# A convolution group by group beside the deformable gathers of the next image

## The chip, the cores and the metric

One core of one Trainium2 chip runs the whole program. The metric is the device time of one execution in microseconds (us); the median of several executions is compared.

## The reference

Four residual layers run over x of shape (4, 64, 128, 128): each adds to x a function of its group norm (32 groups of 2 channels, statistics over one image).

```python
x = x + L0(gn(x), ...)      # attention along columns
x = x + L1(gn(x), ...)      # deformable 3x3 convolution
x = x + L2(gn(x), ...)      # 3x3 convolution whose weights are drawn: w = loc + L eps
x = x + L3(gn(x), ...)      # five steps with position-dependent 3x3 filters
```

The change concerns L1 and L2. L1 computes, by a 3x3 convolution, 27 numbers for each pixel: an offset (dy, dx) and a mask for each of nine taps. Each tap is sampled at its displaced position by bilinear interpolation of four neighbours, and the 9 x 64 samples are contracted with the weight to 64 channels. L2 is an ordinary 3x3 convolution with zero padding, of 64 to 64 channels, plus a bias:

```python
w = weight_loc + einsum('oiab,oib->oia', L, eps_w).reshape(O, I, K, K)
out = conv(x, w, padding='SAME') + b[None, :, None, None]
```

## The kernel before

Everything is float32 here. The program is a sequence of blocks; in each block every engine has its own instruction stream, ordered by semaphores, and between blocks all engines meet at a barrier. `deformable` (L1) and `convolution` (L2) stand one behind the other: `deformable` writes x2 to DRAM, `group_norm(env, 2)` makes scale and shift of each image from the moments, `convolution` reads x2 and writes x3. Each works through the images b = 0 to 3, and each image in G = 32 groups of four image rows (512 pixels).

**The deformable stage.** For each image a table in DRAM holds, for every pixel of the padded image, the channels of two rows and of two columns, so that one gather of 1 KB brings the four neighbours. For each group:

- `params(g)`: TensorE convolves the normalised padded image `dc_xp` with the offset weights (`convolve`, L1292: six matmuls, which the trace lists as twelve passes, since a float32 matmul goes in two) into `dc_pc`; ScalarE copies it out with the bias (L1469); TensorE turns it so that pixels are on partitions (L1516); VectorE makes table indices and weights in 15 small steps (L1588 to L1609), ScalarE the mask (L1472).
- `consume(g)`: GpSimd issues, for each of the four image rows r, nine indirect DMAs (L1447), one per tap, into the row's own buffer `gt[:, r]`. Ahead of rows 0 and 2 stands a one-element addition (`dc_gate`, L1445), behind waits for VectorE's products of the two rows of the group before, whose buffers are filled anew. VectorE multiplies the gathered values with the weights (L1621, one instruction per row, `sampled[r]`). TensorE turns the products back with matmuls against the identity, which also sum the four neighbours (L1529: 20 matmuls a row, 40 in the trace). ScalarE copies the five banks out (L1483), and TensorE contracts them with the filter (L1541, five matmuls, ten in the trace) into `dc_po`. VectorE adds the raw rows of x1 (L1628), takes statistics (L1631, L1633), and SP stores the result to x2 (L1417).

The order is written out by hand in `pairs`: each engine runs `params(g + 1)` ahead of `consume(g)`. For images 1 to 3 the table is made in pieces beside the gathers of the image before: in every second group SP loads raw rows (`dc_nx`, L1380), ScalarE normalises them (L1478), TensorE turns them (L1539), and SP stores the piece (L1398). At a change of image SP loads the next image into `dc_xp` (`load_image`, L1375 and L1376), VectorE normalises it (L1574), and the last group's `consume` follows.

SP's queue in a group holds, in this order: the raw rows of the next group, the wait for the group's output, its store, and in even groups the table's stores and the load of the next piece.

**The convolution.** `bayes_weights` computes the drawn weights in a block of its own. Then whole images are loaded into two padded buffers `cv_xp`, in which partitions 64 to 127 hold the image shifted by one row; ScalarE normalises an image in place (L1782); TensorE convolves group by group into two banks of `cv_po` (L1292); VectorE adds bias and raw rows (L1808) and takes statistics (L1812, L1814); SP loads the raw rows (L1765) and stores x3 (L1769).

## Time and profile before

| | |
|---|---|
| median of 3 runs | 17333.0 us (17320.24 to 17361.81) |
| the profiled execution | 17346.83 us, span 17345.0 us |
| busy in the span | TensorE 73%, weight loads 41%, VectorE 55%, ScalarE 32%, GpSimd 50% |
| mean granted TensorE clock | 0.837 |
| attention and what is ahead of it | up to 6058 us |
| deformable stage | 6061 to 12082 us |
| group norm 2, drawn weights | 12083 to 12123 us |
| convolution | 12124 to 13048 us |
| filters (L3) | 13048 us to the end |

Times are those of one profiled execution, from the start of its span. PE is TensorE, DVE VectorE, ACT ScalarE, POOL GpSimd, SP the engine that only issues DMAs; PEld is the loading of matmul weights. A value in brackets at the end of a row of the timeline is the time that the engine stood idle ahead of it, and what ended that.

### The profile page before, as it was taken

How to read it: one execution, taken by the hardware profiler on the slowest of the kernel's cores; microseconds unless marked ns; L12 is line 12 of the kernel's file. 1: busy time of each engine (PE TensorE's matmuls, PEld its weight loads, DVE VectorE, ACT ScalarE, POOL GpSimd, SP SyncE). 2: the span in 40 equal slices, each digit the busy share in tenths (PEclk: the TensorE clock that was granted, in tenths of full speed). 3: DMA queues.
4: the chain of work that ended last, by engine and by line, in shares of the span. 5: the costliest groups of instructions: out<-in, count | busy, mean ns of one | idle time of the engine just before them, and what ended most of it. 6: DMA issues, size and time to landing. Idle time of an engine off the chain costs nothing. (4 is left out here: it accounts for less than half of the span.)

```text
span 17345.0 us, 233377 instructions
## 1 busy us (share of the span) xinstructions
PE 12681.1 (73%) x80914; PEld 7160.2 (41%) x80914; DVE 9531.3 (55%) x14944; ACT 5526.5 (32%) x7813; POOL 8648.0 (50%) x8027
## 2 busy tenths in 40 slices
PE   5554378888880057767767776776688999999998
PEld 2553145555550045555555555554223333333333
DVE  4556878888883423333333333333126777777777
ACT  1112444444440000000000000000106777777776
POOL 0112411111111057777777777776006777777777
PEclk9999976666665578888888888887899999999999
DMA  4113333333325954454454444333422021110201
GB/s 98 36 28 67 86 60 53 56 54 53 56 50 161 203 149 126 125 135 126 125 139 121 125 125 128 111 110 103 85 60 39 20 49 22 32 37 20 49 21 31
DMA packets 1324675, 1419.97 MB, mean 82 GB/s; under 512 B 514353, under 2 KB 1065537, under 8 KB 1308545
## 3 DMA queue, kind: packets, MB, share of 16 engines
q1 hardware_dynamic: 1031872, 755.61, 21.0%
q0 software_dynamic: 221184, 604.27, 12.1%
q10 hardware_dynamic: 70976, 50.83, 0.9%
q8 instruction: 488, 8.00, 0.2%
q14 instruction: 155, 1.26, 0.0%
HBM read 1049.46 MB, written 276.84 MB: 76 GB/s over the span
## 5 line engine op out<-in xcount | busy, mean ns | idle before, releaser
L1447 POOL DMA_INDIRECT dc_g<-corners,dc_idx x4608 | 4387.1, 952 | 1366.7 <-issue 1326.4
L1529 PE MATMUL dc_ps<-ident,dc_s 128*128 128x128 f32 x20480 | 2861.0, 311 | 1373.2 <-DVE dc_s L1621 1373.2
L2074 POOL TENSOR_TENSOR df_sq<-df_sq 128x512 f32<-128x512 f32 x1920 | 2519.2, 1324 | 1945.3 <-ACT df_sq L2022 1900.1
L1529 PEld LDWEIGHTS dc_ps<-ident,dc_s 128*128 128x128 f32 x20480 | 2813.9, 226 | 1410.8 <-issue 758.9
L2169 DVE SCALAR_TENSOR_TENSOR df_pr<-df_pk,vecs,df_h 128x512 f32<-128x512 f32 x2880 | 2092.8, 742 | 613.1 <-PE df_pk L1963 343.7
L2022 ACT ACTIVATE df_sq<-df_pk,vecs 128x512 f32<-128x512 f32 x2880 | 1936.0, 685 | 979.2 <-DVE df_pr L2169 956.3
L1621 DVE TENSOR_TENSOR dc_s<-dc_g,dc_pt 128x2304 f32<-128x2304 f32 x512 | 1296.5, 2552 | 1652.7 <-DMA dc_g<-corners,dc_idx 1158.6
L756 POOL TENSOR_TENSOR at_md<-at_mt,at_own 64x512 bf16<-64x512 f32 x256 | 327.5, 1279 | 2663.0 <-DVE at_mt L975 2663.0
L1483 ACT ACTIVATE dc_st<-dc_ps 128x512 f32<-128x512 f32 x640 | 327.0, 607 | 4146.6 <-PE dc_ps L1529 4146.6
L1960 PE MATMUL df_pk<-df_t,df_wp 64*128 64x512 f32 x3840 | 1351.0, 641 | 213.9 <-ACT df_sq L2022 156.7
L949 DVE SCALAR_TENSOR_TENSOR at_x<-at_pq,hconst,at_x 128x256 f32<-128x256 f32 x2048 | 1114.7, 617 | 371.9 <-PE at_pq L793 213.9
L1971 PE MATMUL df_py<-df_pr,df_pair 128*64 128x512 f32 x3840 | 1015.5, 669 | 1.7 <-DVE df_pr L2169 1.7
L1628 DVE TENSOR_TENSOR dc_xo<-dc_po,dc_raw 64x512 f32<-64x512 f32 x128 | 87.4, 683 | 1562.3 <-PE dc_po L1541 1562.3
L1960 PEld LDWEIGHTS df_pk<-df_t,df_wp 64*128 64x128 f32 x3840 | 491.0, 188 | 1011.4 <-ACT df_sq L2022 622.2
L1292 PE MATMUL cv_po<-cv_xp,cv_w 128*64 x1536 | 680.7, 600 | 277.1 <-DVE cv_xo L1808 169.0
L1963 PE MATMUL df_pk<-df_t,df_ws 128*128 128x512 f32 x1920 | 875.4, 592 | 0.0
L1004 ACT ACTIVATE at_x<-at_prr 128x512 f32<-128x512 f32 x1024 | 575.5, 597 | 520.3 <-PE at_prr L851 520.3
L982 DVE TENSOR_TENSOR at_x<-at_pt,at_x 128x512 f32<-128x512 f32 x1024 | 673.8, 678 | 108.4 <-PE at_pt L812 104.0
L1292 PE MATMUL dc_pc<-dc_xp,dc_wp 128*32 (+1 forms) x1536 | 692.4, 601 | 43.4 <-DVE dc_base L1576 42.7
L383 PE MATMUL as_py<-wqkv,as_w 64*128 64x128 f32 x2048 | 479.9, 426 | 310.1 <-DVE as_w L423 310.1
L967 DVE TRANSPOSE_TENSOR_REDUCE at_mx<-at_x 128x16 f32<-128x512 f32 x1024 | 687.4, 690 | 0.0
L851 PE MATMUL at_prr<-at_a,at_rel 96*128 96x128 bf16 x4096 | 564.7, 302 | 84.8 <-DMA at_a<-y 52.1
(273 smaller groups left out, 16781.8 us busy)
## 6 DMA issues: line engine op xcount, KB each, us to landing
df_h<-df_h SPq DMA_DIRECT2D x160, 512.0 KB, 7.1
dc_g<-corners,dc_idx POOLq DMA_INDIRECT x4608
corners<-dc_xt SPq DMA_DIRECT2D x90, 512.0 KB, 4.8
at_a<-y SPq DMA_DIRECT2D x192, 192.0 KB
dc_xp<-x SPq DMA_DIRECT2D x32, 1024.0 KB, 20.0
cv_xp<-x SPq DMA_DIRECT2D x8, 4096.0 KB, 49.8
y<-sp_p SPq DMA_DIRECT2D x128, 192.0 KB, 2.8
y<-sp_p SPq DMA_DIRECT2D x64, 384.0 KB, 4.3
```

Source lines behind the costliest of these rows:

```text
L949: last = nc.vector.scalar_tensor_tensor(out=x2, in0=pq[:, t % 2, 256 * i:256 * i + 256].rearrange("p (e b) -> p b e", e=2), scalar=env.hco ...
L967: nc.vector.tensor_reduce(mx[:, q % 2, 16 * t:16 * t + 16], x4.rearrange("p (a c) -> p a c", c=32), AX.X, ALU.max, apply_transpose=True).t ...
L1292: last = nc.tensor.matmul(out, weights[:, i, :], xp[:, bass.ds(row + ky, 4), kx:kx + W], start=(i == 0), stop=(i == 5))
L1447: nc.gpsimd.indirect_dma_start(gt[:, r, k, :, :].rearrange("p a c -> p (a c)"), None, image, bass.IndirectOffsetOnAxis(ap=idx[:, s, r, k:k ...
L1529: t = nc.tensor.matmul(ps[:, j, 128 * r:128 * r + 128], sm[:, r % 2, a, 2 * j:2 * j + 2, :].rearrange("p k c -> p (k c)"), env.ident[:, :] ...
L1621: nc.vector.tensor_tensor(sm[:, r % 2, :, 0:KK, :].rearrange("p a k c -> p k a c"), gt[:, r, :, :, :], w, ALU.mult).then_inc(sampled[r], 1)
L1960: nc.tensor.matmul(pk[:, j % BANKS, :], wp[p, k // 2, :], t[p, n % 2, :], start=True, stop=True, tile_position=(64 * (k % 2), 0)).then_inc ...
L1963: nc.tensor.matmul(pk[:, j % BANKS, :], ws[:, k - 6, :], t[:, n % 2, :], start=True, stop=True).then_inc(tapped, 1)
L1971: nc.tensor.matmul(py[64 * s:64 * s + 64, :], pair[:, :], pr[:, (KK * n + k) % RING, :], start=(k < 2), stop=False, tile_position=(0, 64 * s))
L2022: nc.scalar.activation(sq[:, j % RING, :], pk[:, j % BANKS, :], ACT.Square, bias=env.vecs[:, bias:bias + 1]).then_inc(squared, 1)
L2074: nc.gpsimd.tensor_tensor(a, a, sq[:, (KK * n + other) % RING, :], ALU.add).then_inc(nadded, 1)
L2169: nc.vector.scalar_tensor_tensor(out=rows(pr[:, j % RING, :]), in0=rows(pk[:, j % BANKS, :]), scalar=env.vecs[:, bias:bias + 1], in1=shift ...
```

## The change

- x2 gets 131 rows of DRAM per channel, H + 3: row 0 and the last two hold zeros, stored by twelve DMAs at the head of the deformable stage.
- `bayes_weights` runs ahead of the deformable stage.
- The deformable stage convolves image b - 1 beside the gathers of image b (b = 1 to 3), one group of four rows in each group, from row buffers `cvx` of two times six rows. The outputs use partitions 64 to 127 of `dc_po`, `dc_xo`, `dc_raw` and `dc_now`, of which only 0 to 63 were in use.
- At the end of each image its group norm 2 is computed: VectorE's moments, one matmul, a root on ScalarE, scale and shift on VectorE.
- `convolution` is left with image 3, which it loads and normalises in quarters.
- In `pairs` the first pair of groups of an image is written out ahead of the loop.

```diff
         def pairs(eng, b, params, consume, early=lambda b: None, late=lambda b: None):
             if b == 0:
                 params(0, 0, 0)
-            with eng.Fori(0, NP - 1) as i:
+            params(b, 1, 1)
+            consume(0, 0, 0)
+            params(b, 2, 0)
+            consume(1, 1, 0)
+            with eng.Fori(1, NP - 1) as i:
...
 SP
+            for b in range(B):
+                for y in (0, H + 1, H + 2):
+                    sp.dma_start(x2[b, :, y, :], zero[0:64, 0, :]).then_inc(z_stored, 16)
+                    n += 1
...
+                def load_conv(g, s):
+                    for half in range(2):
+                        sp.dma_start(cvx[64 * half:64 * half + 64, s, :, 1:W + 1],
+                                     x2[bass.ds(b - 1, 1), :, bass.ds(4 * g + half, 6), :].rearrange("o c h w -> (o c) h w")
+                                     ).then_inc(cv_in[s], 16)
+                    sp.dma_start(raw[64:128, s, :], x2[bass.ds(b - 1, 1), :, bass.ds(4 * g + 1, 4), :]
+                                 .rearrange("o c h w -> (o c) (h w)")).then_inc(craw_in[s], 16)
+
+                if b:
+                    for s in range(2):
+                        sp.wait_ge(out_st[s], 16 * b * G // 2)
+                    for s in range(2):
+                        load_conv(s, s)
...
                 def consume(g, s, i):
                     sp.wait_ge(o_out, b * G + g + 1)
...
+                    if b:
+                        sp.wait_ge(cv_out, (b - 1) * G + g + 1)
+                        sp.dma_start(x3[bass.ds(b - 1, 1), :, bass.ds(4 * g, 4), :].rearrange("o c h w -> (o c) (h w)"),
+                                     xo[64:128, s, :]).then_inc(cv_st[s], 16)
+                        if not isinstance(g, int) or g + 2 < G:
+                            load_conv(g + 2, s)
...
 ScalarE, consume
+                    if b:
+                        if isinstance(g, int) and g == 0:
+                            act.wait_ge(gn_ready, b)
+                        act.wait_ge(cv_in[s], 16 * (n - G - s) + 32)
+                        t = nc.scalar.activation(cvx[:, s, :, 1:W + 1], cvx[:, s, :, 1:W + 1], ACT.Identity, bias=gsh2[:, b - 1:b],
+                                                 scale=gsc2[:, b - 1:b])
...
+                        t.then_inc(cv_normed, 1)
...
 TensorE, consume, behind the turning of row r
                         t.then_inc(turned[r], 1)
+                        if r == 1 and b:
+                            pe.wait_ge(cv_normed, n - G + 1)
+                            pe.wait_ge(cv_out, n - G)
+                            convolve(nc, po[64:128, :], wst, cvx[:, s, :, :], 0).then_inc(cv_done, 1)
...
                 pairs(pe, b, params, consume)
+                pe.wait_ge(moments, b + 1)
+                nc.tensor.matmul(pt[:, 416:418], env.gavg[:, :], env.mv[:, b, :], start=True, stop=True).then_inc(summed, 1)
...
 VectorE, consume, behind the product of row 3
+                    if b:
+                        k = n - G
+                        dve.wait_ge(cv_done, k + 1)
+                        dve.wait_ge(craw_in[s], (k - s) * 8 + 16)
+                        dve.wait_ge(cv_st[s], (k - s) * 8)
+                        nc.vector.scalar_tensor_tensor(out=xo[64:128, s, :], in0=po[64:128, :], scalar=bias[64:128, 0:1],
+                                                       in1=raw[64:128, s, :], op0=ALU.add, op1=ALU.add).then_inc(cv_out, 1)
+                        dve.wait_ge(cv_out, k + 1)
+                        dve.wait_ge(cv_kept, k)
+                        nc.vector.bn_stats(now[64:128, s, :], xo[64:128, s, :]).then_inc(cv_stated, 1)
+                        dve.wait_ge(cv_stated, k + 1)
+                        nc.vector.tensor_scalar(st[64:128, b - 1, :][:, bass.ds(g * 6, 6)], now[64:128, s, :], 1.0, None, ALU.mult
+                                                ).then_inc(cv_kept, 1)
                     dve.wait_ge(o_done, n + 1)
...
                 pairs(dve, b, params, consume, late=normalise)
+                dve.wait_ge(kept, (b + 1) * G)
...
+                c.run(nc.vector.bn_aggr(env.mv[0:64, b, :], st[0:64, b, :]))
+                c.run(nc.vector.tensor_copy(env.mv[64:128, b, :], env.mv[0:64, b, :]))
+                c.run(nc.vector.tensor_tensor(gn[:, 0:1], mean, mean, ALU.mult))
+                nc.vector.tensor_tensor(var, var, gn[:, 0:1], ALU.add).then_inc(moments, 1)
+                dve.wait_ge(summed, b + 1)
...
 convolution, for image 3 alone
+            for q in range(4):
+                rows = x2[b, :, 32 * q + 1:32 * q + 33, :]
+                sp.dma_start(xp[0:64, 32 * q + 1:32 * q + 33, 1:W + 1], rows).then_inc(x_in[q], 16)
+                sp.dma_start(xp[64:128, 32 * q:32 * q + 32, 1:W + 1], rows).then_inc(x_in[q], 16)
...
+            for q in range(4):
+                pe.wait_ge(normed, min(3 * q + 6, 12))
+                for i in range(4 * q, 4 * q + 4):
                     for s in range(2):
-                        pe.wait_ge(o_out, b * G + 2 * i)
+                        pe.wait_ge(o_out, 2 * i)
...
 program
-        deformable(env, x1, ins["pgw"], ins["dcw"], table, x2)
-        env.layer_done()
-        group_norm(env, 2)
...
+            bayes_weights(env, ins, wst, bias[:, :])
+            deformable(env, x1, ins["pgw"], ins["dcw"], table, x2, wst, bias, st, gsc2, gsh2, x3)
+            env.layer_done()
+            convolution(env, x2, x3, wst, bias, st, gsc2, gsh2)
```

## Rows read from the trace of the kernel before

**Rows 1.** The page's costliest groups: count, busy us, mean ns, idle before

```profile
L1447 POOL DMA_INDIRECT dc_g<-corners,dc_idx x4608 | 4387.1, 952 | 1366.7 <-issue 1326.4
```

**Rows 2.** Busy us by stretch; last three: TensorE clock, DMA share, GB/s

```profile
6200.00:12060.00 5860.00, 4261.55 (x24418) 3268.27 (x24419) 1915.02 (x3073) 491.84 (x982) 4422.97 (x4852) 0.85 0.44 124
12127.00:12178.00 51.00, 0.00 (x0) 0.00 (x0) 0.06 (x1) 0.62 (x1) 0.00 (x0) 0.50 0.99 174
...
8346.00:8348.00 2.00, 2.00 (x12) 2.00 (x11) 0.00 (x0) 0.00 (x0) 1.70 (x2) 0.50 0.36 115
```

**Rows 3.** Timeline of GpSimd, gates in image 1: start, us, instruction

```profile
8316.77 0.18 POOL L1445 TENSOR_TENSOR dc_gate<-dc_gate 1x1 f32<-1x1 f32 x1
...
8339.35 0.18 POOL L1445 TENSOR_TENSOR dc_gate<-dc_gate 1x1 f32<-1x1 f32 x1
```

**Rows 4.** All gates: min/median/max ns, first and last start

```profile
L1445 POOL TENSOR_TENSOR dc_gate<-dc_gate x256: 182/183/236, 6185.5 to 12037.7; 1x1 f32<-1x1 f32 x128
```

**Rows 5.** Timeline of TensorE in ordinary groups of image 1

```profile
8355.91 5.34 PE L1292 MATMUL dc_pc<-dc_xp,dc_wp 128*32 x12
...
8389.02 6.36 PE L1529 MATMUL dc_ps<-ident,dc_s 128*128 128x128 f32 x40 [4.65 <-DVE dc_s L1621]
```

**Rows 6.** Timeline of TensorE behind the second and third change of image

```profile
9120.87 8.25 PE L1292 MATMUL dc_pc<-dc_xp,dc_wp 128*32 128x512 f32 x12 [14.09 <-DVE dc_base L1576]
...
9161.87 5.34 PE L1292 MATMUL dc_pc<-dc_xp,dc_wp 128*32 x12
...
9202.24 5.34 PE L1292 MATMUL dc_pc<-dc_xp,dc_wp 128*32 x12
...
10638.48 5.34 PE L1292 MATMUL dc_pc<-dc_xp,dc_wp 128*32 x12
...
10677.12 5.34 PE L1292 MATMUL dc_pc<-dc_xp,dc_wp 128*32 x12
```

**Rows 7.** Timeline of VectorE in image 1, the last during an image load

```profile
8311.23 0.68 DVE L1628 TENSOR_TENSOR dc_xo<-dc_po,dc_raw 64x512 f32<-64x512 f32 x1 [12.61 <-PE dc_po L1541]
...
8321.88 5.02 DVE L1621 TENSOR_TENSOR dc_s<-dc_g,dc_pt 128x2304 f32<-128x2304 f32 x2
...
9090.77 2.55 DVE L1621 TENSOR_TENSOR dc_s<-dc_g,dc_pt 128x2304 f32<-128x2304 f32 x1 [18.61 <-DMA dc_g<-corners,dc_idx]
```

**Rows 8.** Timeline of the weights' block and the convolution

```profile
12086.29 0.36 SPq L1669 DMA_DIRECT2D bw_L<-in_l_L  x1
...
12123.61 0.17 DVE L1271 MEMSET cv_xp<- 64x130 f32 x1 [0.92 <-PEq L1661]
...
12177.38 14.85 ACT L1782 ACTIVATE cv_xp<-cv_xp,gsh,gsc 128x16256 f32<-128x16256 f32 x3 [59.00 <-DMA cv_xp<-x]
...
12310.68 10.51 PE L1292 MATMUL cv_po<-cv_xp,cv_w 128*64 x24 [0.94 <-DVE cv_xo L1808]
...
12322.12 8.36 PE L1292 MATMUL cv_po<-cv_xp,cv_w 128*64 x19 [0.94 <-DVE cv_xo L1808]
```

**Rows 9.** All outputs of the convolution: ns, first and last start

```profile
L1808 DVE SCALAR_TENSOR_TENSOR cv_xo<-cv_po,cv_bias,cv_raw x128: 742/743/745, 12225.5 to 13042.2; 64x512 f32<-64x512 f32 x128
```

**Rows 10.** Timeline of the head of the deformable stage

```profile
6062.34 0.62 SPq L1375 DMA_DIRECT2D dc_xp<-x  x1
...
6101.23 15.50 SPq L1391 DMA_DIRECT2D corners<-dc_z  x24
...
6112.54 3.04 DVE L1574 TENSOR_SCALAR dc_xp<-dc_xp,gsc,gsh 128x3968 f32<-128x3968 f32 x3 [7.99 <-DMA dc_xp<-x]
```

**Rows 11.** Groups of instructions at the end of the stage

```profile
L1645 DVE BATCH_NORM_AGGREGATE mv<-dc_stat 64x2 f32<-64x192 f32 x4 | 3.7, 970 | 0.0
```

**Rows 12.** DMA issues, 8113 to 8203: count, KB, median us to landing

```profile
dc_nx<-x SPq DMA_DIRECT2D x2, 128.0 KB, 6.5
```

**Rows 13.** Timeline behind the first change of image, VectorE and GpSimd

```profile
7694.69 5.02 DVE L1621 TENSOR_TENSOR dc_s<-dc_g,dc_pt 128x2304 f32<-128x2304 f32 x2
...
7707.14 0.18 POOL L1445 TENSOR_TENSOR dc_gate<-dc_gate 1x1 f32<-1x1 f32 x1
```

More of the change, by code:

```diff
@@ L1291, in convolve, with deformable @@
         ky, kx = i // 3 * 2, i % 3
-        last = nc.tensor.matmul(out, weights[:, i, :], xp[:, bass.ds(row + ky, 4), kx:kx + W], start=(i == 0), stop=(i == 5))
+        last = nc.tensor.matmul(out, weights[:, i, :], xp[:, row + ky:row + ky + 4, kx:kx + W] if isinstance(row, int) else xp[:, bass.ds(row + ky, 4), kx:kx + W], start=(i == 0), stop=(i == 5))
     return last
-def deformable(env, x1, pgw, dcw, table, x2):
+def deformable(env, x1, pgw, dcw, table, x2, wst, bias, st, gsc2, gsh2, x3):
     nc = env.nc
@@ L1324, in deformable @@
         wp, wd = sb("dc_wp", [128, 6, 32]), sb("dc_wd", [128, 5, C])
-        zero = sb("dc_z", [65, 2, 128])
+        zero = sb("dc_z", [128, 2, 128])
+        cvx = sb("dc_cvx", [128, 2, 6, PW])
+        gn = sb("dc_gn", [128, 4])
         off = sb("dc_off", [128, 512])
@@ L1475, in consume @@
                     n = b * G + g
+                    if b:
[4 more added lines that the diff above has]
+                                                 scale=gsc2[:, b - 1:b])
+                        if isinstance(g, int) and g in (0, G - 1):
+                            t.then_inc(edge, 1)
+                            act.wait_ge(edge, 2 * b - 1 if g == 0 else 2 * b)
+                            y = 0 if g == 0 else 5
+                            t = nc.scalar.activation(cvx[0:64, s, y, 1:W + 1], zero[0:64, 0, :], ACT.Copy)
+                            if g:
+                                t = nc.scalar.activation(cvx[64:128, s, 4:6, 1:W + 1], zero[64:128, :, :], ACT.Copy)
+                        t.then_inc(cv_normed, 1)
                     if more and s == 0:
@@ L1540, in consume @@
                             t.then_inc(piece_turned, 1)
-                        t = nc.tensor.matmul(po[:, :], wd[:, j, :], stt[:, j, :], start=(j == 0), stop=(j == 4))
+                        t = nc.tensor.matmul(po[0:64, :], wd[:, j, :], stt[:, j, :], start=(j == 0), stop=(j == 4))
                     t.then_inc(o_done, 1)
@@ L1555, in _ @@
             c.add(nc.vector.memset(sm[:, :, :, KK, :], 0.0))
+            c.add(nc.vector.memset(cvx[:, :, :, 0:PW:PW - 1], 0.0))
             for r in range(4):
@@ L1627, in consume @@
                     dve.wait_ge(out_st[s], (n - s) * 8)
-                    nc.vector.tensor_tensor(xo[:, s, :], po[:, :], raw[:, s, :], ALU.add).then_inc(o_out, 1)
+                    nc.vector.tensor_tensor(xo[0:64, s, :], po[0:64, :], raw[0:64, s, :], ALU.add).then_inc(o_out, 1)
                     dve.wait_ge(o_out, n + 1)
                     dve.wait_ge(kept, n)
-                    nc.vector.bn_stats(now[:, s, :], xo[:, s, :]).then_inc(stated, 1)
+                    nc.vector.bn_stats(now[0:64, s, :], xo[0:64, s, :]).then_inc(stated, 1)
@@ L1632, in consume @@
                     dve.wait_ge(stated, n + 1)
-                    nc.vector.tensor_scalar(st[:, :, :].rearrange("p b f -> p (b f)")[:, bass.ds(n * 6, 6)], now[:, s, :], 1.0, None, ALU.mult).then_inc(kept, 1)
+                    nc.vector.tensor_scalar(st[0:64, b, :][:, bass.ds(g * 6, 6)], now[0:64, s, :], 1.0, None, ALU.mult).then_inc(kept, 1)
                 pairs(dve, b, params, consume, late=normalise)
-            dve.wait_ge(kept, B * G)
-            c = Steps(dve, link, start + B * G * (PARAM + CONSUME))
@@ L1641, in full_moments @@
+                assert c.n == 7
+                nc.vector.scalar_tensor_tensor(out=gsh2[:, b:b + 1], in0=gn[:, 1:2], scalar=-1.0, in1=gsc2[:, b:b + 1],
+                                               op0=ALU.mult, op1=ALU.mult).then_inc(gn_ready, 1)
+                dve.wait_ge(gn_ready, b + 1)
 def full_moments(env, c, st):
@@ L1644, in full_moments @@
     for b in range(B):
-        c.add(nc.vector.bn_aggr(env.mv[0:64, b, :], st[:, b, :]))
+        c.add(nc.vector.bn_aggr(env.mv[64:128, b, :], st[64:128, b, :]))
     c.wait()
-    c.run(nc.vector.tensor_copy(env.mv[64:128, :, :], env.mv[0:64, :, :]))
+    c.run(nc.vector.tensor_copy(env.mv[0:64, :, :], env.mv[64:128, :, :]))
 def bayes_weights(env, ins, wst, bias):
@@ L1711, in _, with convolution @@
             c.wait()
-def convolution(env, ins, x2, x3):
+def convolution(env, x2, x3, wst, bias, st, gsc2, gsh2):
     nc = env.nc
     G = H // 4
-    x_in = [env.sem("cv_x_loaded0"), env.sem("cv_x_loaded1")]
+    b = B - 1
+    x_in = [env.sem(f"cv_x_loaded{q}") for q in range(4)]
     normed, link, conv_done, o_out, stated, kept = (
@@ L1796, in _ @@
             c = Steps(dve, link)
[L1797 to L1798 removed]
+            clear_borders(nc, xp, c)
             nc.vector.memset(now[:, :, :], 0.0).then_inc(cleared, 1)
             dve.wait_ge(cleared, 1)
[L1801 to L1816 removed]
+            with dve.Fori(0, G // 2) as i:
+                for s in range(2):
+                    n = 2 * i + s
+                    dve.wait_ge(conv_done, n + 1)
+                    dve.wait_ge(raw_in[s], (n - s) * 8 + 16)
+                    dve.wait_ge(out_st[s], (n - s) * 8)
+                    nc.vector.scalar_tensor_tensor(out=xo[64:128, s, :], in0=po[64:128, s, :], scalar=bias[64:128, 0:1],
+                                                   in1=raw[64:128, s, :], op0=ALU.add, op1=ALU.add).then_inc(o_out, 1)
+                    dve.wait_ge(kept, n)
+                    dve.wait_ge(o_out, n + 1)
+                    nc.vector.bn_stats(now[64:128, s, :], xo[64:128, s, :]).then_inc(stated, 1)
+                    dve.wait_ge(stated, n + 1)
+                    nc.vector.tensor_scalar(st[64:128, b, :][:, bass.ds(n * 6, 6)], now[64:128, s, :],
+                                            1.0, None, ALU.mult).then_inc(kept, 1)
+            dve.wait_ge(kept, G)
             full_moments(env, c, st)
```

117 lines of the change are left out of this document (52 added, 65 removed).

## The prediction, made before the change was run

> **What bounds the kernel now.** I read the page first: the costliest group of all is GpSimd's gathers, 4608 of 0.95 us, with 1326 us in which the engine only issued, 0.29 us for each [rows 1]. They fill the deformable stage, 6.2 to 12.06 ms. Busy shares don't tell what sets its pace: TensorE is busy 4262 of 5860 us there, GpSimd 4423 [rows 2]. So next comes the timeline of GpSimd alone. Each half group (two of its four image rows) is opened by a small gate instruction (L1445) and holds 18 gathers; the gates stand 22.58 us apart [rows 3], 45.15 us a group, and 18 x (0.95 + 0.29) with the gate is just that: GpSimd does nothing else and waits for nobody. There are 256 gates from 6185.5 to 12037.7 [rows 4]. I went through all of them: every step has 22.6 us but those at the three changes of image. 255 x 22.58 = 5758 of 5852 us, so each change loses 31. GpSimd's issue is the bound.
>
> How far behind is TensorE? In an ordinary group it stops 4.65 us ahead of its last 40 turning matmuls, for VectorE's product of row 3, which waits for the gathered data [rows 5]. Just behind a change of image it runs without that stop, and its own period can be read: 10638.48 to 10677.12 is 38.6 us, and 9161.87 to 9202.24, a group that also turns a piece of the next table, 40.4 us [rows 6]. So TensorE's chain (offset convolution, ScalarE, turn, VectorE's 15 small steps, product of row 0, 160 turning matmuls, ScalarE's copies, ten matmuls of the filter) has 5 to 6.5 us to spare. VectorE is done with rows 0 and 1 at 8326.90 and GpSimd wants their buffers at 8339.35: 12 us of slack there [rows 3, 7].
>
> Behind the stage nothing overlaps. The weights begin at 12086.3, the convolution's block at 12123.6 [rows 8]; its first output is made at 12225.5, its last at 13042.2 [rows 9]. Two groups take 11.44 us (12310.68 to 12322.12), 5.72 each: twelve passes of TensorE and the handover with VectorE [rows 8].
>
> **The change, part by part.**
>
> *The tail.* Three of four images leave this block; the fourth is loaded in quarters. Such quarters of a padded image are loaded at the head of the deformable stage: issued from 6062.34, VectorE starts on the fourth at 6112.54, 50.2 us later [rows 10]. ScalarE takes 14.85 us for a whole image in three instructions [rows 8], so some 4 for a quarter, and TensorE can start on the first quarters well ahead of that. The raw rows for the addition are issued behind the eight image loads and land with the last, so the first output comes some 51.5 us in. Then 31 x 5.72 = 177, and 1 us of statistics: 230 us. Now it is 13044 - 12123.6 = 920. Saved: **690 us**.
>
> *The weights* move ahead of the deformable stage, where nothing runs beside them either: 37 us there for 37 here, 0. The scales of group norm 2 are made per image inside the stage, so behind it one bn_aggr of 0.97 stands for four [rows 11]: **-3 us**.
>
> *Twelve stores of zero rows* go ahead of the 24 stores of zeros into the tables, on SP, and SP waits for all of them before it stores the first table, for which the first gather waits. 24 take 15.50 us [rows 10]: 12 x 0.65 = **+8 us**, which nothing hides.
>
> *The convolution in the group*, in 96 groups (images 1 to 3 of the gathers). TensorE gets twelve passes between the turning of rows 1 and 2. The offset convolution has as many over 512 columns and takes 5.34 us [rows 5]. TensorE's own period becomes 38.6 + 5.3 = 43.9, to 44.7 as the turning meets the low clock, and 40.4 + 5.3 = 45.7 in every second group of the images that have a table to make. GpSimd stays at 45.15. So the new work fills the stop ahead of row 3 and uses up almost all of TensorE's reserve. Alternating between 45.7 and 44.7 against 45.15 I take 45.27 as the mean: 0.12 x 96 = **+12 us**. The ends: 43.9 everywhere is 0; a chain longer by 0.8 us (seams between the weight loads, the low clock met twice) is 0.8 x 96 = 77.
>
> Of that stop the rows tell one thing more: behind it TensorE gets a granted clock of 0.50 (1.2 GHz), 12 turning matmuls in 2 us [rows 2], and the 40 of row 3 take 6.36 us [rows 5]. Without the stop that time comes back; the periods of 38.6 and 40.4 already have it.
>
> The rest of the new work has cover. VectorE: one addition (0.74 us as in the present block [rows 9]), one bn_stats and one small copy, together about 1.6 us, queued between the product of row 3 and the wait for the filter's matmuls, where it now waits 12.6 us [rows 7]. Uncovered it is 1.6 x 96 = 154. ScalarE: one instruction over 768 columns, 0.7 us by its rate (14.85 / 16256 a column), queued behind the mask and ahead of copies that wait for all four rows. Uncovered, 67. SP: four more issues a group, behind the store of x2; a row buffer is loaded anew as soon as its output is made, two groups (90 us) ahead of use, and the loads most like it land in 6.5 us [rows 12]. Behind them in SP's queue stand the table's stores and the next raw rows, which have as long.
>
> DMA: a group adds 2 x 64 x 6 x 512 B of rows, 131 KB of raw rows and 131 KB of output, 655 KB. The present block loads images at 174 GB/s with a share of 0.99, so this is 3.8 us of all engines in 45, on top of a share of 0.44 [rows 2]. Gathered data lands later by some part of that, but row 3's is wanted 5 us later than now, as the convolution stands ahead of it: 0. The Trainium skill, "DMA: Bandwidth & Descriptors", § Issuing engines are not separate DMA queues, says that DMAs of all issuing engines run on the same 16 engines and interleave. By that rule the row loads get no path of their own, and taken as serial they would add 365 us to the sum. This trace agrees that loads from SP hold gathers up: while an image is loaded a product waits 18.6 us for its data [rows 7].
>
> "SBUF — State Buffer", § Who interferes with whom, in the Trainium skill speaks against more VectorE work beside gathers: some VectorE forms keep GpSimd out of the port by which it writes descriptors. By it the small copy (0.16 us, an estimate) would cost some 15 us in 96 groups. The gates here keep their 22.58 us with VectorE's work between them [rows 3, 7], and the sum takes 0.
>
> *Changes of image.* TensorE no longer goes straight from the filter's matmuls to the next offset convolution; it waits for VectorE's addition, bn_stats, copy, a bn_aggr of 0.97 [rows 11] and three small steps, with its own matmul about 5 us. Queued behind it is the offset convolution of group 1, for which VectorE's rows 0 and 1 of group 0 wait, and for those GpSimd. The root and the scales run beside that convolution. The last group of images 1 and 2 carries a convolution too, 5.3 us. At a change GpSimd's slack is: rows 0 and 1 done at 7699.7, next gate 7707.14, 7.4 us [rows 13]. So nothing at the first change and 5 + 5.3 - 7.4 = 3 us at the others, and 2 us at each of the three for SP's longer queue ahead of the image loads: **+12 us**. Ends: TensorE runs later against GpSimd than now, by up to the 12 us of slack, which each of three image ends could show once (+36); or the image load then meets fewer gathers and the 31 us lost shrink by as much (-36).
>
> **Sum**, on the profiled execution's own 17346.8 us (span 17345.0; 14 us, 0.08%, above the median of the three runs): -690 - 3 + 8 + 12 + 12 = 16686; I say **16685**.
>
> **Rivals.**
> *TensorE becomes the bound.* It has 0 to 1.2 us of reserve left, so any error shows. For it: twelve passes just behind a change of image took 8.25 us in place of 5.34 [rows 6]. Against: here they stand behind 80 turning matmuls, not behind an idle stretch. Worst case 45.2 + 2.9 = 48.1 us a group, 2.95 x 96 = 283: 16970. It decides from 45.15 us on.
> *Gathers land late.* The 3.8 us of row traffic push each group, 3.8 x 96 = 365: 17050. For it: the 18.6 us at an image load [rows 7]. Against: an image load drives the share to 0.99 [rows 2]; here it is about 0.52.
> *Slower than before.* Normalised rows come late, and TensorE, which works in order, holds the turning of rows 2 and 3 behind the convolution's wait. The stage may lose 673 + 12 = 685 us before the gain is gone, 685 / 96 = 7.1 us in each group. For that a load must land about 100 us after its issue; the nearest takes 6.5 [rows 12]. At 10 us a group it is 17620.
>
> **How the numbers follow.** 0.80 for the forecast (GpSimd still sets the pace, at most 0.8 us a group, changes of image within their bounds: 16630 to 16800), 0.12 for TensorE as the bound by 0.8 to 3 us a group (16780 to 16970), 0.05 for late gathers, 0.02 for slower, 0.01 for no change. Low end: no loss in the groups and changes of image that gain, 16686 - 12 - 36, about 16635. High end: into TensorE as the bound by 1.8 us a group, 16850. That leaves out less than 2 in 10. Under about 0.3% (50 us) nothing can be told from no change here: faster 0.97, same 0.01, slower 0.02.
>
> **What would show it.** Gates still 22.6 us apart in images 1 to 3, the stop ahead of row 3 gone or under 1 us, twelve passes of about 5.3 us behind row 1, a last block of about 230 us, the first gate some 45 us later (weights and zeros). Gates further apart without waits for data mean TensorE; with VectorE waiting for gathered data, the DMA. TensorE waiting for ScalarE ahead of the convolution would be the slow case. The forecast is wrong above all if TensorE's chain has a link that the present stop hides.

## The result, and the profile after

The changed kernel takes 16673.96 us (median of 5 runs, the kernel before beside it 17336.88). The ratio is 0.9609, 95% interval 0.9597 to 0.9621: 3.9% faster. The forecast was 16685 us, within 16630 to 16850. One of the five executions, the one that was profiled, took 20178.76 us with a granted TensorE clock of 0.55 from 7000 to 12000 us (0.89 in f1_again); the ratio leaves it out, and the median of the other four is 16666.2 us.

The rows below are therefore of the same kernel in the run f1_again: median 16675.42 us, the profiled execution 16677.81 us, span 16675.9, mean granted clock 0.847.

The costliest groups of the page. GpSimd's gathers stand as in [rows 1]; behind the bar are busy time, mean ns of one, and the idle time before them.

```profile
L1485 POOL DMA_INDIRECT dc_g<-corners,dc_idx x4608 | 4384.5, 951 | 1367.0 <-issue 1322.6
L1583 PE MATMUL dc_ps<-ident,dc_s 128*128 128x128 f32 x20480 | 2697.2, 300 | 1030.3 <-DVE dc_s L1682 1030.2
```

All gates of the stage, against [rows 4]: first start 53.2 us later, 5865.1 us from first to last in place of 5852.2.

```profile
L1483 POOL TENSOR_TENSOR dc_gate<-dc_gate x256: 182/183/253, 6238.7 to 12103.8; 1x1 f32<-1x1 f32 x128
```

The timeline of GpSimd in image 1 of the gathers: 22.52 us from gate to gate; the gate ahead of these stands at 8327.86, 22.62 earlier, so the step is that of [rows 3].

```profile
8350.48 0.18 POOL L1483 TENSOR_TENSOR dc_gate<-dc_gate 1x1 f32<-1x1 f32 x1
...
8373.00 0.18 POOL L1483 TENSOR_TENSOR dc_gate<-dc_gate 1x1 f32<-1x1 f32 x1
```

The timeline of TensorE over the same groups, against [rows 5]: start, duration, instruction, and in brackets the idle time ahead of it. L1583 turns the rows, L1292 into dc_po is the new convolution, L1599 is the filter, L1292 into dc_pc the offset convolution.

```profile
8322.99 5.34 PE L1292 MATMUL dc_pc<-dc_xp,dc_wp 128*32 x12
...
8336.28 10.96 PE L1583 MATMUL dc_ps<-ident,dc_s 128*128 128x128 f32 x80 [6.10 <-DVE dc_s L1682]
8347.16 5.37 PE L1292 MATMUL dc_po<-dc_cvx,cv_w 128*64 128x512 f32 x12
8352.46 9.20 PE L1583 MATMUL dc_ps<-ident,dc_s 128*128 128x128 f32 x80
8362.34 4.51 PE L1599 MATMUL dc_po<-dc_st,dc_wd 128*64 128x512 f32 x10 [0.69 <-ACT dc_st L1535]
8366.78 5.34 PE L1292 MATMUL dc_pc<-dc_xp,dc_wp 128*32 x12
```

The convolution takes 5.37 us and waits for nothing. The stop of 4.65 us ahead of row 3 is gone: rows 2 and 3 are 80 matmuls in one piece, 9.20 us, where the 40 of row 3 alone took 6.36 [rows 5]. In some groups a stop is left, of up to 1.4 us but for the image loads and the end of the stage:

```profile
10243.15 4.73 PE L1583 MATMUL dc_ps<-ident,dc_s 128*128 128x128 f32 x40 [1.36 <-DVE dc_s L1682]
```

The granted clock over rows 2 and 3 is full, in place of the 0.50 of [rows 2]. Stretches of the trace: length, busy time of PE, PEld, DVE, ACT and POOL, then clock, DMA share and GB/s:

```profile
6238.00:12150.00 5912.00, 4625.61 (x25649) 3259.70 (x25647) 2093.24 (x3427) 596.95 (x1106) 4431.64 (x4864) 0.88 0.50 134
...
8352.50:8361.50 9.00, 9.00 (x81) 8.96 (x80) 4.03 (x4) 0.00 (x0) 6.87 (x8) 1.00 0.37 107
```

VectorE still waits for row 3's gathered data, 6.77 us here, but in this group TensorE no longer waits for the product of row 3. It still waits 6.10 us for that of row 0, which is part of its own chain. VectorE's three new instructions lie in the time in which it waits for the filter (12.61 us in [rows 7], 10.12 now, behind them).

```profile
8352.19 2.55 DVE L1682 TENSOR_TENSOR dc_s<-dc_g,dc_pt 128x2304 f32<-128x2304 f32 x1 [6.77 <-DMA dc_g<-corners,dc_idx]
8354.78 0.76 DVE L1689 SCALAR_TENSOR_TENSOR dc_xo<-dc_po,cv_bias,dc_raw 64x512 f32<-64x512 f32 x1
8355.57 0.69 DVE L1693 BATCH_NORM_STATS2 dc_now<-dc_xo 64x6 f32<-64x512 f32 x1
8356.43 0.33 DVE L1695 TENSOR_SCALAR cv_stat<-dc_now 64x6 f32 x1 [0.17 <-DVE dc_now L1693]
8366.89 0.68 DVE L1702 TENSOR_TENSOR dc_xo<-dc_po,dc_raw 64x512 f32<-64x512 f32 x1 [10.12 <-PE dc_po L1599]
```

The head of the stage on SP's queue, against [rows 10]: the zero stores, now 12 + 24, take 12.76 + 10.74 = 23.5 us in place of 15.5.

```profile
6146.31 12.76 SPq L1402 DMA_DIRECT2D x<-dc_z  x12
6159.11 10.74 SPq L1408 DMA_DIRECT2D corners<-dc_z  x24
```

The last block, against [rows 8, 9]: its start, the first two groups' passes (24) behind the second quarter's normalisation, the two raw loads, and the first output, 49.8 us in.

```profile
12150.09 0.65 SPq L1840 DMA_DIRECT2D cv_xp<-x  x1
...
12181.05 13.36 PE L1292 MATMUL cv_po<-cv_xp,cv_w 128*64 128x512 f32 x24 [34.06 <-ACT cv_xp L1864]
...
12187.62 6.54 SPq L1845 DMA_DIRECT2D cv_raw<-x  x2
...
12199.89 0.76 DVE L1889 SCALAR_TENSOR_TENSOR cv_xo<-cv_po,cv_bias,cv_raw 64x512 f32<-64x512 f32 x1 [47.95 <-DMA cv_raw<-x]
```

```profile
L1889 DVE SCALAR_TENSOR_TENSOR cv_xo<-cv_po,cv_bias,cv_raw x32: 756/756/758, 12199.9 to 12374.8; 64x512 f32<-64x512 f32 x32
```

From the block's first load to its last statistic (12376.7) it is 226.6 us; before it was 920.

### The profile page after: what moved, and what is told of

Same layout as the page of the kernel before. It is cut to its first block and busy times, and to the rows that moved or that the text cites. A ratio compares the mean times of both kernels' runs of the same rounds, so it can differ in the third digit from the quotient of the medians.

```text
span 20176.9 us, 232645 instructions
## 1 busy us (share of the span) xinstructions
PE 16509.0 (82%) x80920; PEld 8538.1 (42%) x80920; DVE 9630.5 (48%) x14967; ACT 5613.2 (28%) x7926; POOL 8569.6 (42%) x8027
## 5 line engine op out<-in xcount | busy, mean ns | idle before, releaser
L1583 PE MATMUL dc_ps<-ident,dc_s 128*128 128x128 f32 x20480 | 3892.6, 382 | 781.6 <-DVE dc_s L1682 781.6
L1583 PEld LDWEIGHTS dc_ps<-ident,dc_s 128*128 128x128 f32 x20480 | 3833.8, 296 | 930.7 <-issue 822.9
L2041 PE MATMUL df_pk<-df_t,df_wp 64*128 64x512 f32 x3840 | 1596.6, 840 | 56.5 <-ACT df_sq L2103 39.5
L2052 PE MATMUL df_py<-df_pr,df_pair 128*64 128x512 f32 x3840 | 1347.4, 874 | 0.8 <-DVE df_pr L2250 0.8
L2044 PE MATMUL df_pk<-df_t,df_ws 128*128 128x512 f32 x1920 | 1309.9, 825 | 0.0
L1292 PE MATMUL dc_pc<-dc_xp,dc_wp 128*32 (+1 forms) x1536 | 1145.8, 924 | 43.3 <-DVE dc_base L1637 42.6
L1599 PE MATMUL dc_po<-dc_st,dc_wd 128*64 128x512 f32 x1280 | 953.8, 919 | 57.0 <-ACT dc_st L1535 57.0
L1292 PE MATMUL dc_po<-dc_cvx,cv_w 128*64 128x512 f32 x1152 | 843.1, 909 | 0.0
L2044 PEld LDWEIGHTS df_pk<-df_t,df_ws 128*128 128x128 f32 x1920 | 410.5, 214 | 787.4 <-issue 768.1
L2160 POOL TENSOR_TENSOR df_pr<-df_pr 128x512 f32<-128x512 f32 x320 | 405.9, 1269 | 781.6 <-DVE df_pr L2250 778.9
```

The costliest lines, as they stand in the source:

```text
L1292: last = nc.tensor.matmul(out, weights[:, i, :], xp[:, row + ky:row + ky + 4, kx:kx + W] if isinstance(row, int) else xp[:, bass.ds(row + ...
L1583: t = nc.tensor.matmul(ps[:, j, 128 * r:128 * r + 128], sm[:, r % 2, a, 2 * j:2 * j + 2, :].rearrange("p k c -> p (k c)"), env.ident[:, :] ...
L1599: t = nc.tensor.matmul(po[0:64, :], wd[:, j, :], stt[:, j, :], start=(j == 0), stop=(j == 4))
L2041: nc.tensor.matmul(pk[:, j % BANKS, :], wp[p, k // 2, :], t[p, n % 2, :], start=True, stop=True, tile_position=(64 * (k % 2), 0)).then_inc ...
L2044: nc.tensor.matmul(pk[:, j % BANKS, :], ws[:, k - 6, :], t[:, n % 2, :], start=True, stop=True).then_inc(tapped, 1)
L2052: nc.tensor.matmul(py[64 * s:64 * s + 64, :], pair[:, :], pr[:, (KK * n + k) % RING, :], start=(k < 2), stop=False, tile_position=(0, 64 * s))
```

## The experiments

A kernel and the one before were always timed on one chip, and three chips were used. On two of them, those of the runs e1 to e4 and g1 to g4, every trace has pauses of TensorE between short matmuls, and the kernel before took 20.4 ms in place of 17.35 (it has no trace there), so times of these sets are compared within their set only. The kernel before had a median of 20428.93 us beside the e runs, 17351.06 beside the f runs, 20377.5 beside the g runs.

### How much TensorE has to spare: e1 to e4, then f1 to f3

The convolution of a group is six matmuls, twelve passes. One, eight or twelve matmuls take their place. These kernels leave matmuls out or add some in twice, so their x3 is another sum; only their times are of use:

```diff
-                            convolve(nc, po[64:128, :], wst, cvx[:, s, :, :], 0).then_inc(cv_done, 1)
+                            order = (0,)    # or (0, 1, 2, 3, 4, 5, 1, 2), or (0, 1, 2, 3, 4, 5) * 2
+                            for q, j in enumerate(order):
+                                ky, kx = j // 3 * 2, j % 3
+                                t = nc.tensor.matmul(po[64:128, :], wst[:, j, :], cvx[:, s, ky:ky + 4, kx:kx + W],
+                                                     start=(q == 0), stop=(q == len(order) - 1))
+                            t.then_inc(cv_done, 1)
```

> The changed kernel once more, unchanged, for its profile. If GpSimd's issue still sets the pace of the deformable stage: 16640 to 16700 us, gates 22.6 us apart in images 1 to 3 and no stop of TensorE ahead of row 3. If TensorE has become the bound: the same time, but gates 22.8 us or more apart, with GpSimd idle ahead of each gate for VectorE's products.

> The convolution beside the gathers is one matmul (its first) in place of six; loads, normalising, addition and stores stay. If GpSimd sets the pace and six matmuls just fit: 15 to 25 us faster than the changed kernel (12 for the groups, the rest at the changes of image). If TensorE is the bound by 0.8 us a group or more: over 77 us faster. If late gathered data were the cost: no gain at all, since the traffic stays.

> Eight matmuls in place of six (matmuls 1 and 2 are added in twice, so x3 is another sum): 1.8 us more of TensorE in each of 96 groups. If the reserve is used up by six: 47.0 us a group in images 1 and 2 and 46.3 in image 3, about +140 us on the changed kernel. If a reserve of over 2 us is left: +0 to 20 us. If TensorE was the bound already: the full 1.8 x 96 = +171 us.

> Twelve matmuls in place of six (x3 holds twice the convolution): 5.3 us more of TensorE in each of 96 groups. By the same chain: 5.3 x 64 + 4.6 x 32 - 12 = about +475 us on the changed kernel; with TensorE as the bound already +513; with 2 us of reserve left about +320.

Measured: 19537.32, 19604.22, 19648.14 and 20182.09 us; ratios to the kernel before 0.9567 (0.9529 to 0.9605), 0.9603 (0.9565 to 0.9642), 0.9604 (0.9568 to 0.9640) and 0.9873 (0.9834 to 0.9912). The first three can't be told apart. The traces show why they can't be read as meant. In e1_again TensorE pauses for up to 1.7 us between single turning matmuls, marked as issue, so with no engine to wait for. Now and then it also waits far longer than in f1_again for ScalarE's copies of the turned rows (12.30 us in the last row, 0.69 to 0.84 there):

```profile
9993.89 0.37 PE L1583 MATMUL dc_ps<-ident,dc_s 128*128 128x128 f32 x1 [1.03 <-issue]
...
10000.25 0.37 PE L1583 MATMUL dc_ps<-ident,dc_s 128*128 128x128 f32 x1 [1.73 <-issue]
...
13292.80 5.98 PE L1599 MATMUL dc_po<-dc_st,dc_wd 128*64 128x512 f32 x10 [12.30 <-ACT dc_st L1535]
```

A group takes 67 us there, whether it has a convolution or not: the 64 gates of an image span 2113 us in image 0 of the gathers, which has none, and 2103 to 2141 in images 1 to 3; with one matmul (e2_one_matmul) it is 2135, and 2127 to 2163. Only with twelve (e4_twelve_matmuls) do images 1 to 3 grow, to 2302 to 2350 us beside 2139 in image 0. So GpSimd's issue is not the bound on this chip, the six matmuls cost nothing there either, and the set says nothing of a reserve beside GpSimd. The change gains 892 us by the medians, 200 more than its last block saves; where these come from stays open, as there is no trace of the kernel before with such pauses. Three of the kernels were run again on a chip without such pauses.

> The changed kernel unchanged, again for its profile and as the control of this set. In e1 the deformable stage of all kernels, the one before too, was held up by TensorE's own issue (pauses of 0.3 to 2.4 us between turning matmuls), which the trace of before didn't have. Without these pauses: 16640 to 16700 us, gates 22.6 us apart in images 1 to 3 and no stop ahead of row 3, if GpSimd sets the pace; gates 22.8 us or more apart if TensorE does. With these pauses: 19500 us.

> One matmul of the convolution in place of six in each group. Without pauses of TensorE's issue: 15 to 25 us faster than the control if GpSimd sets the pace and six just fit, over 77 us faster if TensorE is the bound. With pauses: no difference, as in e2.

> Twelve matmuls in place of six. Without pauses: +475 us on the control if six use up the reserve, +513 if TensorE was the bound already, +320 if 2 us of reserve are left; gates about 25 us apart in each case.

Measured: 16675.42, 16657.49 and 17087.0 us; ratios 0.9609 (0.9595 to 0.9622), 0.9601 (0.9588 to 0.9615), 0.9848 (0.9835 to 0.9861). With one matmul in place of six the kernel gains 18 us of 16675 and no more: the convolution is hidden. The 15 to 25 us expected came true, but not by its terms, which had 12 us for the groups. The gates within an image keep 22.57 us in both kernels; the whole difference lies at the changes of image (second step of images 2 and 3 22.6 and 24.4 us, 26.4 in f1_again; last step of images 0 to 2 31.3, 28.3 and 28.0 us, and 34.2, 32.1 and 31.2). TensorE's timeline in f2_one_matmul shows the stop ahead of row 3 back where the convolution had filled it:

```profile
8327.11 4.73 PE L1583 MATMUL dc_ps<-ident,dc_s 128*128 128x128 f32 x40 [2.05 <-DVE dc_s L1687]
...
8372.33 6.36 PE L1583 MATMUL dc_ps<-ident,dc_s 128*128 128x128 f32 x40 [4.26 <-DVE dc_s L1687]
```

With six matmuls more, TensorE is the bound. The timelines of TensorE and GpSimd in f3_twelve_matmuls:

```profile
10729.00 10.51 PE L1593 MATMUL dc_po<-dc_cvx,cv_w 128*64 128x512 f32 x24
```

```profile
10743.90 0.18 POOL L1483 TENSOR_TENSOR dc_gate<-dc_gate 1x1 f32<-1x1 f32 x1
...
10769.64 0.18 POOL L1483 TENSOR_TENSOR dc_gate<-dc_gate 1x1 f32<-1x1 f32 x1 [3.19 <-DVE dc_s L1687]
...
10792.54 0.18 POOL L1483 TENSOR_TENSOR dc_gate<-dc_gate 1x1 f32<-1x1 f32 x1
```

The convolution grew by 10.51 - 5.37 = 5.14 us in 96 groups, the kernel by 411.6, 4.29 us a group. By the times TensorE's reserve with six matmuls is 5.14 - 4.29 = 0.85 us. By the gates within images 1 to 3, which leave the changes of image out, a group takes 49.5, 49.8 and 49.5 us; less 5.14 and against 45.15 that is a reserve of 0.8, 0.5 and 0.8. So it is 0.5 to 0.9 us; the expectations had 0 and 2 us at their ends. Every second gate now waits for VectorE's products of rows 0 and 1, and these, through the steps ahead of them, for TensorE's turned offset convolution.

### The head and the tail trimmed: f4

The twelve zero-row stores go behind the first table's stores with a semaphore of their own. In the last block a raw load goes behind each of the first two quarters, not both behind the fourth, and TensorE starts three of the four pairs of groups of a quarter as soon as that quarter is normalised:

```diff
-            for b in range(B):
-                for y in (0, H + 1, H + 2):
-                    sp.dma_start(x2[b, :, y, :], zero[0:64, 0, :]).then_inc(z_stored, 16)
...
+                if b == 1:
+                    sp.wait_ge(edge_stored, 16 * 3 * B)
...
+                if q < 2:
+                    load(q, q)
...
-                pe.wait_ge(normed, min(3 * q + 6, 12))
...
+                    pe.wait_ge(normed, 3 * q + 3 if i % 4 < 3 else min(3 * q + 6, 12))
```

> The changed kernel with two edits. The twelve stores of zero rows go behind the stores of the first table, with a semaphore of their own (they are needed by image 1 only): 8 us faster if they were on the way to the first gather. In the last block the first two loads of raw rows go behind the first quarter of the image instead of behind all four, and TensorE starts on a quarter as soon as that one is normalised: its first output comes 26 us into the block instead of 51, 25 us faster. Together -33 us on the control; if the first output was set by something else than the queue of loads, only -8.

Measured: 16655.24 us, ratio 0.9597 (0.9584 to 0.9610), 20 us below f1_again. It beats both kernels, by less than expected. The head gave its 8 us (from group norm's start to the first gate 162.7 us, and 171.3 in f1_again). The tail gave 10 of 25 (the last output stands 214.7 us into the block, and 224.7 in f1_again). VectorE's timeline there: the first output comes 26.7 us into the block, but the third stands at 51.4.

```profile
12147.92 0.76 DVE L1891 SCALAR_TENSOR_TENSOR cv_xo<-cv_po,cv_bias,cv_raw 64x512 f32<-64x512 f32 x1 [24.88 <-PE cv_po L1292]
...
12172.54 0.76 DVE L1891 SCALAR_TENSOR_TENSOR cv_xo<-cv_po,cv_bias,cv_raw 64x512 f32<-64x512 f32 x1 [17.78 <-DMA cv_raw<-x]
```

SP's queue in the same stretch gives the reason. The store of the first output is issued only behind all of the image's loads, and the raw load of the third group behind that store. Of the ten loads six take 5.5 to 6.5 us to issue.

```profile
12148.88 5.67 SPq L1851 DMA_DIRECT2D cv_xp<-x  x1
...
12160.65 5.35 SPq L1846 DMA_DIRECT2D x<-cv_xo  x1
12166.23 0.51 SPq L1841 DMA_DIRECT2D cv_raw<-x  x1
```

### Order of loads, place of the convolution, traffic: g1 to g4

g2 puts the convolution behind row 3. g3 loads every row buffer a second time, into a buffer that nothing reads. g4 is the trimmed kernel with the raw rows of the last block in four quarters:

```diff
 g2
-                        if r == 1 and b:
+                        if r == 3 and b:
 g3
+                        sp.dma_start(cvy[64 * half:64 * half + 64, s, :, 1:W + 1],
+                                     x2[bass.ds(b - 1, 1), :, bass.ds(4 * g + half, 6), :].rearrange("o c h w -> (o c) h w")
+                                     ).then_inc(cv_in[s], 16)
...
-                        act.wait_ge(cv_in[s], 16 * (n - G - s) + 32)
+                        act.wait_ge(cv_in[s], 32 * (n - G - s) + 64)
 g4, against f4
-                if q < 2:
-                    load(q, q)
-            ahead(sp, load, store)
+                sp.dma_start(raw[64:128, q, :], rows.rearrange("c h w -> c (h w)")).then_inc(raw_in[q], 16)
+            with sp.Fori(0, G // 2) as i:
+                store(2 * i, 0)
+                store(2 * i + 1, 1)
```

Two of the expectations below count 192 groups with a convolution. There are 96, so the prices they add up by the group are half as high: some 200 us for the rival of g2, and for that of g3 235 us at half a load and 48 at 0.5 us a group.

> The changed kernel itself again, the reference line for the three beside it. 16675 us, and 16660 to 16690.

> The image's convolution is issued behind the turning of row 3 instead of row 1, just ahead of the filter's five matmuls; nothing else differs, and all of the output is computed. Theory (the group's length is set by GpSimd's gathers, and TensorE has about 1 us to spare): the place is indifferent, each gate stays at 22.6 us, within 10 us of the control; the stop of 0.7 us that TensorE makes for ScalarE's first copy ahead of the filter goes under the convolution, so TensorE's own period falls from some 44 to some 43.3 us, which the time does not show. Rival (VectorE hands each group's rows out in step with TensorE, and a turning of row 0 that comes 5.4 us late holds the next product and the next gate): some 2 us or more a group, 192 groups with a convolution, +400 us.

> Each row buffer of the convolution is loaded a second time, into a buffer that nothing reads, and ScalarE waits for both: 192 KB... twice 384 KB a group pair in place of once; all of the output is computed. Theory (the row loads are hidden: DMA engines have room beside the gathers, and the buffers are loaded a whole pair of groups ahead): gates stay at 22.6 us, within 10 us of the control. Rival (the gathers share the DMA engines with the loads, and their landing moves the group): a load takes about 4.9 us to land, and if half of that reaches the gathers of each of 192 groups the kernel is 470 us slower; already a tenth of it, 0.5 us a group, would be +95 us.

> The trimmed kernel, and in its last block the raw rows come in four loads of a quarter of the image, each behind that quarter's rows, in place of a load for each group. Theory (the third output of the trimmed kernel stood at 51.4 us because its raw rows queued behind the image's loads): the outputs now run 5.7 us apart from the first at about 27 us, so the last stands 27 + 31 x 5.7 = 204 us into the block instead of 215, and the kernel is 10 us faster than the trimmed one, 16645 us, 30 us below the control. Rival (the queue of the transfers themselves, not the order, holds the block: the raw rows delay the image's quarters): as the trimmed kernel, 16655 us, or slower.

This set fell on a chip with pauses again: 19557.33, 19707.17, 19565.26 and 19574.16 us; ratios 0.9593 (0.9565 to 0.9622), 0.9641 (0.9597 to 0.9685), 0.9601 (0.9572 to 0.9630), 0.9604 (0.9569 to 0.9639). None can be told from g1_again by its interval.

*g3.* Twice the row traffic moved the time by 8 us, within the spread, which would not show 48 us either. The DMA share of the stretch 8500 to 12500 went from 0.34 (g1_again) to 0.38 (g3_double_loads):

```profile
8500.00:12500.00 4000.00, 2570.28 (x11965) 1741.95 (x11963) 964.21 (x1613) 298.45 (x537) 2018.06 (x2228) 0.77 0.34 95
```

```profile
8500.00:12500.00 4000.00, 2574.18 (x12006) 1736.35 (x12006) 964.70 (x1596) 293.50 (x528) 2021.28 (x2231) 0.78 0.38 100
```

The groups are 67 us long there, so late gathers would have had more cover than at 45; the run speaks against a cost of 235 us and more but doesn't settle the rival alone.

*g2.* 150 us slower than g1_again by the medians, but its runs reach from 19477 to 19736 and the intervals overlap, so the times alone don't tell. The traces lean towards the rival: from first to last gate images 1 to 3 take 2198, 2195 and 2180 us, and 2134, 2126 and 2138 in g1_again, 1.8 us more a group, though image 0, which has no convolution, differs by 36 us too. For a chip without pauses the place of the convolution stays open. The trace shows something else. In groups without a piece of the next table, the filter's matmuls start before the convolution ends:

```profile
8735.42 4.08 PE L1292 MATMUL dc_po<-dc_cvx,cv_w 128*64 128x512 f32 x9
8738.91 0.64 PE L1599 MATMUL dc_po<-dc_st,dc_wd 128*64 128x512 f32 x1
8739.33 0.59 PE L1292 MATMUL dc_po<-dc_cvx,cv_w 128*64 128x512 f32 x1
8739.39 0.59 PE L1599 MATMUL dc_po<-dc_st,dc_wd 128*64 128x512 f32 x1
...
8740.25 3.17 PE L1599 MATMUL dc_po<-dc_st,dc_wd 128*64 128x512 f32 x7
8743.34 5.34 PE L1292 MATMUL dc_pc<-dc_xp,dc_wp 128*32 x12
```

The 22 passes take 8743.34 - 8735.42 = 7.92 us from the first start to the start of what follows; apart they take 5.30 + 4.44 = 9.74 by the same measure in f1_again (8347.16 to 8352.46, 8362.34 to 8366.78).

*g4.* The last block has no pauses even on this chip (32 outputs from 15037.3 to 15211.4 in g1_again, 174.1 us, and 174.9 in f1_again), so it can be read. The theory fell. The last output stands 236 us into the block (14951.52 to 15187.5), not 204, and 215 in f4_trim. The third output now waits 35.6 us, for the store of the first, by VectorE's timeline:

```profile
15022.17 0.76 DVE L1878 SCALAR_TENSOR_TENSOR cv_xo<-cv_po,cv_bias,cv_raw 64x512 f32<-64x512 f32 x1 [35.59 <-DMA x<-cv_xo]
```

SP's queue: the raw quarters lengthen it, and the first stores go out at 15011, 31 us behind the first output.

```profile
15004.94 5.71 SPq L1838 DMA_DIRECT2D cv_raw<-x  x1
15011.02 1.33 SPq L1831 DMA_DIRECT2D x<-cv_xo  x2
```

The rival was right that the raw rows lengthen the queue: SP is through with the last image load 53 us into the block, and 39 us in f4_trim. But the third output waits by the order all the same, since the stores stand behind every load. What holds the tail behind its first output is that loads and stores share one queue in which most loads take 5.5 to 10.5 us to issue. A version whose stores leave from another engine's queue was not tried, so that this would free them is not shown. By its median f4_trim is the fastest kernel that was run.

## Why the prediction was right

**The terms.** Worked out from the profile of before and that of f1_again:

| part | predicted | measured |
|---|---|---|
| unchanged code ahead of the stage | 0 | +9 |
| weights moved to the head | +37 | +36 |
| zero rows | +8 | +8.0 |
| groups | +12 | -1 |
| changes of image | +12 | +14 |
| behind the last gate, up to the last block | -40 | -39.6 |
| last block | -690 | -694 |
| whole | -661 | -669 |

They are read so. From the start of group norm (6067.4; 6058.5 before, where the code ahead is the same) to the first gate it is 171.3 us, 44.3 more than before, 8.0 of them the zeros. First to last gate is 12.9 us more, split below. From the last gate to the last block it is 46.3 us in place of 85.9, and that block is 226.6 in place of 920.4. The whole is the difference of the spans.

*The tail.* The first output came at 49.8 us (51.5 predicted, by the head's loads of [rows 10]), and 31 more by 174.9 us (177). Both sizes held.

*The bound.* GpSimd's issue still sets the pace: its gathers' busy and idle times are those of before within 3 us, and the gates stand 22.57 us apart by their median in every image (22.58 in [rows 3]). Twelve passes took 5.37 us as the offset convolution does; the 8.25 us feared of [rows 6] did not come: none of the convolution's 1152 passes took over 0.65 us. That it stands behind 80 busy turning matmuls is the reason given in the prediction; no run varied it here.

*The groups* are the one term of the sum that was mis-sized, by 13 us. I took 45.7 us for TensorE in groups with a piece of the table. f3_twelve_matmuls, where TensorE is the bound, gives its period: 64 gates in 1558.5, 1568.7 and 1559.7 us (63 steps of images 1 to 3), 49.5 to 49.8 a group, less 5.14 is 44.3 to 44.7 as the mean over groups with and without a piece. For image 3, which makes no table, 43.9 to 44.7 had been predicted, and groups with a piece were no longer than those without: TensorE's offset convolutions start 49.7 and 49.6 us apart in image 1 of f3_twelve_matmuls (medians). The reserve of 0.5 to 0.9 us is there, and so the groups cost nothing.

*The changes of image* came to 14 us where 12 was said, but only half of that is sure. The second step of images 2 and 3 is 26.4 in place of 22.6 us, 3.8 us twice, where 3 was predicted from GpSimd's slack of 7.4 [rows 13]; image 1, ahead of whose change no convolution runs, has no such step, as predicted. The last step of images 0 to 2, in which the next image is loaded, is 34.2, 32.1 and 31.2 us (29.8, 31.4 and 30.5 before): 5.8 us in all, where 2 each had been taken. That and 0.8 us in the steps across the change make 14; the other steps are 1 us shorter than before. In f4_trim, which has the same code there, the second steps are 26.4 and 25.6 us, but the last ones 30.1, 31.4 and 30.7, as before. So some 7 us for the convolution at the second step repeat, and the 5.8 us put down to SP's longer queue do not: that they agree with the 6 of the sum was luck.

*Small sizes.* ScalarE's instruction for the convolution's rows took 1.02 us where 0.7 had been worked out, and the row loads landed in 4.9 us (median) where 6.5 was taken. Both are hidden.

*The gathers.* Row 3's data is waited for as before (VectorE's waits for gathered data are 1158.6 us in all before and 1073.0 now), and TensorE's idle time ahead of turning fell from 1373 to 1030 us. The DMA share of the stage rose from 0.44 [rows 2] to 0.50 while the gates kept their distance. The Trainium skill, "DMA: Bandwidth & Descriptors", § Issuing engines are not separate DMA queues, says that the transfers share 16 engines; that sharing cost the group nothing that could be measured, since data was late only where somebody had time to wait. By "SBUF — State Buffer", § Who interferes with whom, in the Trainium skill VectorE's small copy could have held up the gathers; their mean went from 952 to 951 ns, so no run here shows it.

*The rivals.* TensorE as the bound did not come true, and f3_twelve_matmuls shows how near it was. Late gathers: the gates keep 22.57 us, and doubled loads at 67 us a group show no cost above the spread. Normalised rows late: the convolution waits for nothing in f1_again.

## What to carry to other kernels

Work that runs by itself behind a long stage is worth its whole time when it fits under that stage's bound. Read how long each engine's own chain is where nothing holds it up, for instance behind a hiccup, and not its share of busy time: TensorE's 73% hid a reserve of some 6 us, and the moved work took 5.4 of them. Then ask what the smallest remaining reserve is (0.5 to 0.9 us here), because nearly all of the next addition will be paid for (411.6 of 493 us in f3_twelve_matmuls). When a block is short, the order of loads and stores on one queue decides it more than the arithmetic: in f4_trim the first store waited 13 us behind loads, and 31 us in g4 once more loads had been put ahead.

## What the runs showed of the hardware

- The granted clock of the turning matmuls went with the stop ahead of them, but not by its length alone. In f2_one_matmul the 40 behind a stop of 2.05 us took 4.73 us, at full clock, and the 40 behind 4.26 us took 6.36, at a mean of 0.73. In the same trace 40 behind 1.93 us took 6.36 and 40 behind 3.60 us took 4.73. Busy times, clock, DMA share and GB/s of the first two stretches, then TensorE's timeline at the other two:

```profile
8327.00:8331.80 4.80, 4.69 (x40) 4.54 (x40) 1.78 (x4) 0.00 (x0) 3.61 (x4) 1.00 0.37 109
8372.30:8378.70 6.40, 6.36 (x40) 6.17 (x40) 1.68 (x3) 0.00 (x0) 4.88 (x6) 0.73 0.36 106
```

```profile
9440.00 4.73 PE L1583 MATMUL dc_ps<-ident,dc_s 128*128 128x128 f32 x40 [3.60 <-DVE dc_s L1687]
...
10523.60 6.36 PE L1583 MATMUL dc_ps<-ident,dc_s 128*128 128x128 f32 x40 [1.93 <-DVE dc_s L1687]
```

- Filling the stop gave back more than the stop itself. Over the stage TensorE's idle time ahead of turning fell by 343 us (1373.2 to 1030.3), 3.6 for each of the 96 groups, and the turning itself got 164 us shorter (2861.0 to 2697.2 busy), 1.7 for each.
- On two of three chips TensorE paused, mostly for 0.2 to 1.8 us, between single 128-column matmuls, and the deformable stage was half as long again (2113 us for the gates of image 0 in e1_again, 1434 in f1_again). The convolution's passes over 512 columns mostly ran without pauses (twelve in 5.37 us in e1_again), but not always; in g2_behind_row3 they have some too, in the row below. The last block kept its length. What the pauses come from was not settled.

```profile
9014.74 1.82 PE L1292 MATMUL dc_po<-dc_cvx,cv_w 128*64 128x512 f32 x2 [1.51 <-issue]
```
- Matmuls of the convolution and of the filter write different halves of the output partitions (64 to 127 and 0 to 63), and where they follow one another directly the records of g2_behind_row3 overlap: 22 passes in 7.92 us in place of 9.74.
